# Splitting layer 1's streamed expert weights one matrix a step, and three smaller moves around the attention of layer 1

## The reference, cut to what matters

```python
xn = _layernorm(x)
x = x + _L0_attn_ref(xn, ...) + _L0_ffn_ref(xn, ...)     # sigmoid attention; 32 experts of 64, top 4, one shared of 128
xn = _layernorm(x)
x = x + _L1_attn_ref(xn, ...) + _L1_ffn_ref(xn, ...)     # softmax attention with relative positions; 16 experts of 176, top 4, one shared of 352
# _L1_attn_ref: softmax((q k^T + position term) / sqrt(8)) v for 16 heads of 8, then a projection
# _L1_ffn_ref:  y = sum_e w_e * down_e(silu(gate_e x) * up_e x), w_e = 0 for the experts that were not chosen; plus the shared expert
```

## Time and profile before

| what | value |
|---|---|
| median of 3 runs (lowest, highest) | 1137.98 us (1134.75, 1138.6) |
| profiled execution: its own time, and its span from first to last instruction | 1134.96 us, 1133.0 us |
| busy in the span: PE, DVE, ACT, POOL | 1026.2, 757.1, 728.0, 541.2 us |
| granted TensorE clock, mean over the span | 0.967 of full speed |

### The profile page before, as it was taken

The page is one execution under the profiler, slowest core; times in us unless marked ns, Lnnn a source line. Parts: engine busy times, 40 slices in busy tenths (PEclk is TensorE's granted clock), DMA queues, the critical chain, the costliest instruction groups (busy, mean ns, idle before and its releaser), DMA issues. The chain is left out here.

```text
span 1133.0 us, 22305 instructions
## 1 busy us (share of the span) xinstructions
PE 1026.2 (91%) x7828; PEld 641.8 (57%) x7828; DVE 757.1 (67%) x1707; ACT 728.0 (64%) x1087; POOL 541.2 (48%) x707
## 2 busy tenths in 40 slices
PE   3899999999999469999999899999999878999997
PEld 2444444777776334555554445555444556878785
DVE  7235341777865476887788788777785257676766
ACT  1699987555546137777777677777776555545453
POOL 1377775665644122333455533344222276655564
PEclk9999999999999658999999999999999899999999
DMA  4541231536466596888888888888771574343342
GB/s 161 190 128 62 84 98 55 160 115 189 140 179 198 192 254 195 243 241 240 244 260 254 235 245 240 240 245 240 217 220 40 128 226 121 122 118 121 118 122 92
DMA packets 146430, 197.41 MB, mean 174 GB/s; under 512 B 33292, under 2 KB 113149, under 8 KB 146285
## 3 DMA queue, kind: packets, MB, share of 16 engines
q1 hardware_dynamic: 126254, 184.32, 52.4%
q0 software_dynamic: 20064, 11.66, 6.1%
HBM read 123.00 MB, written 72.74 MB: 173 GB/s over the span
## 5 line engine op out<-in xcount | busy, mean ns | idle before, releaser
L1090 DVE TENSOR_REDUCE a_part<-a_duo 128x2 f32<-128x1024 f32 (+3 forms) x256 | 215.3, 855 | 14.1 <-PE a_duo L963 12.6
L755 POOL DMA_DIRECT2D scr_y1c<-ys x240 | 118.9, 504 | 204.1 <-DVE ys L1071 201.2
L1083 DVE CUSTOM_DVE_ANT_0 a_band_sum<-a_duo,a_rel_raw 128x256 f32<-128x256 f32 (+2 forms) x320 | 131.4, 447 | 84.2 <-PE a_duo L963 64.3
L1529 POOL TENSOR_TENSOR f_hid_lo<-f_hid,att 128x512 fp32r<-128x512 f32 (+1 forms) x100 | 129.4, 1297 | 106.8 <-ACT att L1498 106.8
L976 PE MATMUL a_duo<-att 32*128 32x512 f32 (+3 forms) x672 | 139.2, 410 | 21.1 <-DVE a_part L1090 12.9
L963 PE MATMUL a_duo<-att 31*128 31x512 f32 (+3 forms) x672 | 145.4, 428 | 9.0 <-DVE a_part L1090 4.1
L706 ACT ACTIVATE a_probs<-a_duo 128x1024 f32<-128x1024 f32 x192 | 139.9, 829 | 14.1 <-PE a_duo L655 12.7
L1043 ACT ACTIVATE a_rel<-a_rel_ps 128x384 f32<-128x384 f32 x240 | 117.5, 490 | 48.3 <-PE a_rel_ps L950 47.7
L1661 DVE TENSOR_TENSOR f_hid<-f_u,w_share 128x512 f32<-128x512 f32 (+1 forms) x168 | 116.3, 692 | 27.5 <-POOL f_hid_lo L1529 4.6
L644 POOL TENSOR_TENSOR a_probs<-a_probs,const 128x256 f32<-128x256 f32 x128 | 101.5, 809 | 48.8 <-ACT a_probs L706 48.6
L1529 POOL TENSOR_TENSOR f_hid_lo<-f_hid,f_hid_hi 128x512 fp32r<-128x512 f32 x68 | 88.0, 1294 | 76.0 <-ACT f_hid_hi L1498 76.0
(11 more groups left out here) (268 smaller groups left out, 2048.1 us busy)
## 6 DMA issues: line engine op xcount, KB each, us to landing
a_rel_raw<-scr_rel SPq DMA_DIRECT2D x128, 384.0 KB, 4.5
scr_rel<-a_rel SPq DMA_DIRECT2D x120, 384.0 KB, 3.7
w_share<-scr_cw SPq DMA_DIRECT2D x144, 128.0 KB, 3.2
w_share<-scr_cw SPq DMA_DIRECT2D x44, 256.0 KB, 3.3
scr_y1c<-ys POOLq DMA_DIRECT2D x240, 8.0 KB, 3.7
w_share<-scr_cw SPq DMA_DIRECT2D x20, 192.0 KB, 2.8
w_share<-scr_cw SPq DMA_DIRECT2D x16, 224.0 KB, 3.0
att<-scr_q SPq DMA_DIRECT2D x36, 96.0 KB
```

What stands on the lines that cost most here:

```text
L755: eng.dma_start(scr["y1c"][w, b, head, :, at:at + T // 4], sb["ys"][32 * (2 * hd + c) + HD * w:32 * (2 * hd + c) + HD * (w + 1), h % 2, :] ...
L1083: ins = dve.tensor_tensor_reduce(band_sum[:, m % 2, hd, 0:wide], both[:, hd, (a - 4 * x) * P:(b - 4 * x) * P], rel_raw[:, e % RING, hd, (a ...
L1090: ins = dve.tensor_reduce(part[:, h % 2, x, :, j % 4], both[:, :, lo * P:hi * P], AX.X, ALU.max, negate=True)
L1529: pool.tensor_tensor(hid_lo[0:m, n % 4, :], hid[0:m, n % 2, :], f32(hid_hi[0:m, n % 4, :]), ALU.subtract).then_inc(lo_ready, 1)
```

## The change

Four things are changed.

1. In layer 1's experts the split of a group is no longer done in one piece. Step 1 + 3g + m handles matrix m of group g, on POOL behind that step's `hid_lo`, on ACT one step later, behind the high part of `hid`. The semaphores count matrices now (3 for a group), so SP's load of a group, and PE's first use, wait for three counts in place of one. The steps at which SP loads groups stay.
2. The first row of maxima (h = 0) is stored by ACT's queue, ahead of ACT's copy in slot -4; all others stay with SP.
3. POOL's twelve loads of pairs 2 and 3 wait for the first turned scores (`st_ready` 1, slot 0) in place of the eighth score block.
4. In the last block of layer 0, the logits of the last block but one are computed right behind `turn`, in place of right ahead of the last block's logits.

```diff
+        def store_rows(eng, h):
+            pair, x = h // 2, h % 2
+            eng.wait_ge(row_saved, h + 1)
+            for hd in range(2):
+                to = 32 * (2 * (pair % 2) + hd) + MROW
+                eng.dma_start(f32(qs[to:to + 1, home(pair), x * HALF:(x + 1) * HALF]),
+                              f32(rows_sb[64 + 4 * hd:68 + 4 * hd, h % 2, :])).then_inc(row_stored[h % 2], 16)
...
-                if m % 8 == 7 and 0 <= m < SLOTS:
...
+                if m % 8 == 7 and 8 <= m < SLOTS:
+                    store_rows(sp, m // 8)
...
-            pool.wait_ge(s_ready, 8)
+            pool.wait_ge(st_ready, 1)
...
                 r = n + LR
+                if n + LS == 10:
+                    store_rows(act, 0)
...
-        split_at = {(1 + GRP * g if EARLY else starts[g - 2]): g for g in range(0 if EARLY else 2, len(groups))}
+        split_at = {1 + GRP * g + m: (g, m) for g in range(len(groups)) for m in range(3)}
...
                 if n >= 2:
-                    sp.wait_ge(raw_lo, n - 1)
+                    sp.wait_ge(raw_lo, 3 * (n - 1))
...
                 if n in starts[:-1]:
-                    pe.wait_ge(raw_lo, starts.index(n) + 1)
+                    pe.wait_ge(raw_lo, 3 * (starts.index(n) + 1))
...
+                    if k == 0 and name == "turn" and ti == NC - 1:
+                        logits(y_ps[1], NC - 2)
                     if k == 0 and name == "logits":
-                        logits(y_ps[1], NC - 2)
                         logits(y_ps[1][:, 4 * L1.E:], NC - 1).then_inc(logits_ready, 1)
...
-                if n in split_at:
-                    split(split_at[n])
...
+                if n - 1 in split_at:
+                    split_hi(act, *split_at[n - 1])
...
-                if n in split_at:
-                    split_lo(pool, split_at[n])
                 if n < M:
...
+                if n in split_at:
+                    split_lo(pool, *split_at[n])
```

More of the change, by code:

```diff
@@ L1139, in experts @@
         GRP = 3
-        starts = [*range(EARLY, K, GRP), K] if EARLY else [0, 1, *range(3, K, GRP), K]
+        starts = [*range(EARLY, K, GRP), K]
         groups = list(zip(starts, starts[1:]))
-        split_at = {(1 + GRP * g if EARLY else starts[g - 2]): g for g in range(0 if EARLY else 2, len(groups))}
-        load_at = {(1 + GRP * g if EARLY else starts[g - 2]): g for g in range(2, len(groups))}
+        split_at = {1 + GRP * g + m: (g, m) for g in range(len(groups)) for m in range(3)}
+        load_at = {1 + GRP * g: g for g in range(2, len(groups))}
         if EARLY < K:
@@ L1261, in load @@
                             sp.dma_start(dst, d[f"{name}_{k}"][:, a:b]).then_inc(raw_loaded[s], 16)
-            if k == 0 and not EARLY:
-                next(weights_loaded(weights, d, sp, [raw], P))
             for g in range(min(2, len(groups))):
@@ L1328, in raw_count, with split_hi, split_lo @@
             return sum(len(pieces(m, *groups[g])) for g in range(n % 2, n + 1, 2) for m in range(3))
-        def split_hi(eng, n, copy):
+        def split_hi(act, n, m):
             c0, c1 = groups[n]
[L1332 to L1335, removed]
+            act.wait_ge(raw_loaded[n % 2], 16 * raw_count(n))
+            for rows, a, b in pieces(m, c0, c1):
+                ins = act.activation(w_hi[m][0:rows, a - EARLY * P:b - EARLY * P], raw[0:rows, n % 2, m, a - c0 * P:b - c0 * P], ACT.Copy)
             ins.then_inc(raw_hi, 1)
-        def split_lo(eng, n):
+        def split_lo(pool, n, m):
             c0, c1 = groups[n]
[L1340 to L1344, removed]
+            pool.wait_ge(raw_hi, 3 * n + m + 1)
+            for rows, a, b in pieces(m, c0, c1):
+                ins = pool.tensor_tensor(w_lo[m][0:rows, a - EARLY * P:b - EARLY * P], raw[0:rows, n % 2, m, a - c0 * P:b - c0 * P],
+                                         f32(w_hi[m][0:rows, a - EARLY * P:b - EARLY * P]), ALU.subtract)
             ins.then_inc(raw_lo, 1)
@@ L1468, in _ @@
         def _(act):
[L1469 to L1474, removed]
             if k == 0:
@@ L1519, in _ @@
                 pool.memset(ecol24[:], 0.0).then_inc(zeroed, 1)
-            if not EARLY:
-                split_lo(pool, 0)
-                split_lo(pool, 1)
             for n in range(M + TAIL):
-                if n in split_at:
-                    split_lo(pool, split_at[n])
                 if n < M:
```

## The result

The changed kernel takes 1123.88 us (median of 4 runs, 1120.99 to 1128.17), the kernel before 1137.32 (4 runs beside it, 1134.75 to 1138.6): a ratio of 0.9888, 95% interval 0.9851 to 0.9925, 13.4 us less. Forecast were 1120 us and a gain of 16. From the starts of the blocks in the two traces: the block of the attention begins 0.8 us earlier, takes 3.8 more (501.5 against 497.7), and the experts from chunk 0 to the end of the span take 9.7 less (233.7 against 243.4). So all of the gain is in the experts, and the attention, in this execution, lost part of it.

The account below looks back on a forecast made before the run. Bound: PE, losing 18 us in the first column block of layer 1's experts, plus a 4.75 us attention wait. Splits 12.8 plus row and loads 3.2, logits 0, make 16.0 us less: 1120 forecast, range 1116 to 1123 (57%).

Parts of the forecast that it names:

- The bound: Layer 1's experts, first column block: 69.2 us against 51.1 at PE's pace, so 18 us lost and within reach.
- the forecast 14.3 us: Layer 1's experts: chunk 25 starts at 944.55 in place of 958.81, before 1.5 us are given back for DMA.
- Part 1, POOL's pace: First column block: POOL sets the pace, one `hid_lo` and one split, 2.27 us a step against PE's 2.10, 18 steps.
- lies across this: POOL's paced steps: one thing interrupts them, DVE's reciprocal in step 17, 3.34 us.
- The clock falls in the paced stretch: Rival, 3%: PE's pauses bring 1.2 GHz, steps of 3.9 us; 10 such steps eat the 16 us, 18 give 1149.
- Part 1, the DMA: Experts' weight loads: SP's later loads make ACT wait for weights; 1.5 us back, bounds 0 and 4.
- late weights stay the bound: Rival, 15%: SP's later loads make ACT wait for groups 3 and 5; part 1 brings about 7, total 1125.
- Parts 2 and 3: Layer 1's attention, first row's wait: 4.75 less 0.6 for ACT's issue and 0.9 for table load, 3.2 us less.
- The table load: ACT behind slot 0: 1.28 us, hidden in the old wait, comes to light and costs 0.9 us.
- Part 4: Layer 0's last block: logits fill PE's 5.89 us layer-norm pause; gain zero, a higher clock worth up to 2 not counted.
- the choice between 1119.0 and 1122.0: Whole kernel: 16.0 off the profiled execution's 1134.96 gives 1119.0, against the median 1137.98 gives 1122.0; 1120 given.
- the row's wait stays or moves: Rival, 17%: first row lands at 419 again, or wait moves to slot 6 or 8; parts 2 and 3 bring 0.

Follow-up runs that it names:

- e1_split_only: The changed kernel with the first row on SP, the loads after the eighth score block and the logits in their old place; 1127.34 us, ratio 0.9923.
- e12_after_again: The changed kernel once more, without an edit, for a second profile; 1121.48 us, ratio 0.9878.
- e8_fill: The changed kernel with all rows on SP, the cast in step 22, an early Exp, and 25 full-height matmuls between slots -11 and 2; ratio 0.9895.
- e11_best: The changed kernel with the two 1 MB loads in SP's step 14, the cast in DVE's step 22 and the first row on SP; 1127.24 us, ratio 0.9917.
- e10: The changed kernel with the two 1 MB loads in SP's step 14 and the cast of f_wp in DVE's step 22; ratio 0.9897.
- e9_load_14: The changed kernel with the two 1 MB loads of the attention result moved from SP's step 9 to 14; ratio 0.9931.

## Why the prediction was right, and where its sizes were off

**The bound** was read rightly: the first column block of layer 1's experts had the time to give, and part 1 gave it. Of the forecast 14.3 us, 10.2 came in the profiled execution (69.2 - 59.0), 9.3 and 9.1 in e1_split_only and e12_after_again (by chunk 24's gate, 68.0 less 58.7 and 58.9). With the DMA's 1.5 taken back, part 1 was put at 12.8 us, between 10 and 15; from chunk 0 to the end of the span it measured 9.7, 9.4 and 9.0, so it came out below its own lower bound. The mechanism was right and its size too large.

**Part 1, POOL's pace.** Right to 2%: 2.24 us a step for 2.27; the second low part comes 5.56 us after chunk 0 for 5.6. Mis-sized is the sentence that nothing but the reciprocal "lies across this". A cast of 0.44 us that I had not counted became 4.28 and opened POOL's gap of 2.59 us. The lower clock behind it opened 0.73 more: this is the mechanism of the rival "The clock falls in the paced stretch" (3%), on some eight matmuls in place of ten steps. These 3.3 us and the 0.6 by which the reciprocal's gap is longer (1.39 for 0.8), less 0.5 for the faster pace, make 3.4 of the missing 4.1. Of the last 0.7, PE's wait for `hid_lo(19)` at 944.97 is 0.4, since POOL makes the last two pieces of a split (1.38 us) ahead of it; the rest isn't assigned.

**Part 1, the DMA.** I took 1.5 us back, between 0 and 4, and put it at ACT's wait for weights. In the first trace ACT waits 0.25 us, and DVE 0.59 and 0.28 for `share`, which I had left out; in the second, of the same program, ACT waits 0.73 and 1.10 and DVE 2.22 and 1.76. So the transfers have no slack there, as the late cast and the moved loads show too. Of three things that want the DMA engines, `share` is the one that is late the longest. The rival "late weights stay the bound" was named after the wrong transfer, though in size its mechanism is real.

**Parts 2 and 3.** Slot 0 was forecast 4.1 us earlier (4.75 - 0.6) and came 3.6 earlier; the first exponentials, behind the table load, were forecast 3.2 earlier and came 2.6 earlier (25.4 us after the block's start, 28.0 before). It came by part 3 alone (4.8 us by itself), and part 2 costs 1.0 to 1.2, not 0.6: PE waited 1.57 us for the copy, so that ACT's issue was hardly hidden. Part 2 was a mistake. The table load came to light as forecast, 1.28 us between slot 0 and the first exponentials; moving it away gave the wait to PE. The rule of the Trainium skill (DMA: Bandwidth & Descriptors) on issuing engines, which I named as a rival's ground, held for part 2; the rival as a whole fell, since the row came in time.

**Part 4.** The pause is 4.66 us for 5.89, and the clock behind it as low as before. Zero, as forecast, though no run has this part alone.

**The clock in the attention** is what I had left out altogether. Over nine profiles with the loads moved, the block is 0.44 us longer for each us by which the clock rises later. Less 0.45 us for each us to the rise, they give 473.8 to 475.4; the three with the loads in place 475.8, 477.6 and 479.4 (left out are e8_fill and e11_best, whose clock fell again for some 10 us; shorter falls, of 3 to 7 us, in the profiles of before, of the changed kernel and of e10 are left in, and taking them out changes the difference by less than 0.2). Between the means, 474.7 and 477.6, lie 2.9 us. So the slot's gain seems to stay until the block's end once the clock is taken out, though with three profiles on one side, which differ by 3.6, this is an estimate. When the rise comes seems to differ by chance: the same program showed 35.0 and 60.3. The 19.6 us by which it came later than in the profile of before are worth 19.6 x 0.45 = 8.8 us, more than parts 2 and 3 together.

**The whole.** The forecast of 16 us less stands against 13.4, whose interval (a ratio of 0.9851 to 0.9925) is 8.5 to 17 us. That 1120 came within 4 us is in part luck: part 1 was 3 us too large, the choice between 1119.0 and 1122.0 another 2, and the clock's rise moves one execution by 10. The median of 1123.88 even lies just outside the 1116 to 1123 to which I had given 57%, at the 1122 to 1125 of the rival "the row's wait stays or moves", which did not happen; the second median, 1121.48, lies inside. The time alone could not decide between them, but the rows do: PE waits for no row.

## What to carry to other kernels

When a stall goes, look which transfers and which small instructions had lain in its shadow. Here one small cast took ten times as long beside a filled GpSimd, and behind this stood a DMA wait of the same size, so that removing the cast's stall paid nothing. And before a moved transfer is credited with a gain, count what else stands in the same DMA engines at its new place: with the two 1 MB loads moved, the experts took 4 to 6 us more. And part 2, a move to another queue that waits for the same engines, cost 1 us that only the runs with one part at a time brought out.

## What the runs showed of the hardware that I had not expected

- DVE's cast of 128x128 took 4.26 to 4.31 us in five profiles beside a GpSimd without gaps, and 0.43 to 0.69 in the nine where GpSimd had gaps or a boundary came soon; each long one ended 0.1 us after GpSimd had run dry. The 1 MB loads are ruled out as its cause (e9_load_14). ACT's splits, which the change moved too, were not tested by themselves. The Trainium skill (SBUF — State Buffer, "SBUF: two separate sides") says that DVE in a two-port mode and GpSimd take a shared pair of ports as an exclusive lock for a whole instruction. That fits a wait of up to one GpSimd instruction, 1.3 us; why DVE did not get its turn for three to four of them is not settled here, and whether this cast is in such a mode no run shows.
- In the attention, where many of the matmuls have 31 or 32 rows, PE's granted clock stayed at 1.2 GHz for the first 34 to 60 us, and the time of the rise differed by 25 us between two executions of the same program. Seven added matmuls of 128 rows were followed by a rise and, 3.6 us on, a fall; six more by none.
- Twelve loads from GpSimd's queue kept transfers of 2 KB in SP's and in ACT's queue waiting alike: 10.6 us from issue to landing in the one, 12.0 in the other. With the loads moved away the same transfer took less than 5.7 us in SP's queue.
